# Transposes two tiles behind and loads one step ahead, in three stages of an adaLN block with local attention and a soft mixture

## The reference

```python
h = _layernorm(x) * (1 + ca) + sa
x = x + ga * _L0_attn_ref(h, w_qkv, proj, w_out, b_out)   # window of 7 tokens, ends in out @ w_out + b_out
h = _layernorm(x) * (1 + cb) + sb
x = x + gb * _L0_ffn_ref(h, gamma_x, gamma_slot, slot_embeds, w1, w2)

# _L0_ffn_ref, one batch entry: s = 2048 tokens, d = 1024, e*t = 4096 slots
xn = rms_norm(x, gamma_x)
se = rms_norm(slot_embeds, gamma_slot)
logits = jnp.einsum('bsd,etd->bset', xn, se)
dispatch = jax.nn.softmax(logits, axis=1)                 # over the tokens
slots = jnp.einsum('bsd,bset->betd', xn, dispatch)
processed = jax.nn.gelu(slots @ w1, approximate=False) @ w2
combine = jax.nn.softmax(logits.reshape(b, s, e * t), axis=-1)   # over the slots
out = jnp.einsum('bnd,bsn->bsd', processed.reshape(b, e * t, d), combine)
```

## Time and profile before

| | us |
|---|---|
| two executions | 3873.7 and 4113.04 |
| their median | 3993.37 |
| the profiled execution | 3893.19 |
| span of its slowest core (core 1) | 3891.6 |
| spans of the other cores | 3852.0 to 3878.8 |
| TensorE busy, core 1 | 2578.9 (66%) |
| VectorE, ScalarE busy, core 1 | 966.6 (25%), 626.4 (16%) |

### The profile page before, as it was taken

The page is one execution under the profiler, slowest core; times in us unless marked ns, Lnnn a source line. Parts: engine busy times, 40 slices in busy tenths (PEclk is TensorE's granted clock), DMA queues, the critical chain, the costliest instruction groups (busy, mean ns, idle before and its releaser), DMA issues. The chain is left out here.

```text
span 3891.6 us, 33138 instructions; the slowest of 8 cores (3852.0 to 3891.6 us)
## 1 busy us (share of the span) xinstructions
PE 2578.9 (66%) x11776; PEld 1192.4 (31%) x11776; DVE 966.6 (25%) x1998; ACT 626.4 (16%) x1213; POOL 547.2 (14%) x1021
## 2 busy tenths in 40 slices
PE   5227665656545656665665649888849999667677
PEld 0213222222212222222222213333314444334444
DVE  0543333324652222222222210000041000123232
ACT  0100221211211111111111102222200000122221
POOL 5000000000001111011110115555520000000000
PEclk6558666656767786778777769999969999878788
DMA  9131212002211111111111152222272323132322
GB/s 143 43 68 22 44 38 44 27 33 65 79 54 41 41 41 38 31 41 41 41 39 30 41 99 69 66 65 66 69 141 65 87 65 87 55 119 76 119 76 76
DMA packets 138943, 241.76 MB, mean 62 GB/s; under 512 B 34967, under 2 KB 80279, under 8 KB 137758
## 3 DMA queue, kind: packets, MB, share of 16 engines
q0 software_dynamic: 78864, 138.49, 15.6%
q1 hardware_dynamic: 59918, 101.16, 8.6%
HBM read 201.85 MB, written 83.89 MB: 73 GB/s over the span
## 5 line engine op out<-in xcount | busy, mean ns | idle before, releaser
L1140 PE MATMUL pH<-slots_fm,w_bf 128*128 128x512 bf16 x2048 | 461.0, 385 | 98.2 <-DMA h_sp<-hbuf 54.4
L1227 PE MATMUL pP<-w_bf,hblk 128*128 128x512 bf16 x2048 | 457.7, 385 | 36.8 <-DVE w_bf L1205 20.8
L1054 PE MATMUL pDs<-xn_tm,atm 128*128 128x512 bf16 x1024 | 303.6, 469 | 30.2 <-DVE atm L1045 30.2
L971 PE MATMUL pL<-xn_fm,sefs 128*128 128x512 bf16 x1024 | 289.1, 452 | 50.6 <-DVE sefs L961 50.6
L98 POOL DMA_DIRECT2D h_sp<-hbuf x512 | 272.0, 539 | 287.2 <-ACT hbuf L1151 276.6
L1140 PEld LDWEIGHTS pH<-slots_fm,w_bf 128*128 128x128 bf16 x2048 | 198.1, 99 | 360.8 <-issue 138.7
L1227 PEld LDWEIGHTS pP<-w_bf,hblk 128*128 128x128 bf16 x2048 | 199.3, 98 | 296.3 <-issue 62.0
L98 POOL DMA_DIRECT2D L_sp<-lch x256 | 136.3, 541 | 947.2 <-ACT lch L1005 912.2
L996 ACT ACTIVATE ach<-pL,colC,rscale_all 128x512 bf16<-128x512 f32 x128 | 97.8, 773 | 901.4 <-DVE colC L985 901.4
L1362 PE MATMUL pO<-proc_sm,w_smb 128*128 128x512 bf16 x1024 | 225.4, 381 | 0.9 <-DVE w_smb L1347 0.9
L1036 PE MATMUL pAt<-ident_bf_s,ach 128*128 128x128 bf16 x512 | 52.1, 263 | 239.9 <-DVE atm L1045 239.9
(11 more groups left out here) (184 smaller groups left out, 2484.5 us busy)
## 6 DMA issues: line engine op xcount, KB each, us to landing
L_sp<-lch POOLq DMA_DIRECT2D x256, 128.0 KB, 3.0
h_sp<-hbuf POOLq DMA_DIRECT2D x512, 64.0 KB, 1.8
lblk<-L_sp SPq DMA_DIRECT2D x8, 4096.0 KB, 16.6
se_st<-slot_embeds POOLq DMA_DIRECT2D x32, 512.0 KB, 3.5
wsl<-wmod POOLq DMA_DIRECT2D x96, 128.0 KB, 8.0
xst<-x SPq DMA_DIRECT2D x16, 512.0 KB, 3.2
xrs<-x SPq DMA_DIRECT2D x16, 512.0 KB, 3.8
x_sp<-x2b POOLq DMA_DIRECT2D x16, 512.0 KB, 4.6
```

Source lines behind the costliest of these rows:

```text
L971: e.matmul(pL[nb][:, 0:512], se_fs[buf][:, j * 128:(j + 1) * 128], xn_fm[:, j * N + nb * 512:j * N + (nb + 1) * 512], start=(j == 0), stop ...
L1054: e.matmul(pDs[half][:, 0:512], a_tm[buf][:, nt * 128:(nt + 1) * 128], xn_tm[:, nt * D + half * 512:nt * D + half * 512 + 512], start=(nt ...
L1140: e.matmul(pH[pbase + q][:, 0:512], w1_bf[:, j * HID + hc * 128:j * HID + (hc + 1) * 128], slots_fm[:, j * S + hf * 2048 + q * 512: j * S ...
L1227: e.matmul(pP[2 * (st % 2) + half][:, 0:512], h_blk[blk % 2][:, hc * HBW + st * 128: hc * HBW + (st + 1) * 128], w2_bf[:, hc * D + half * ...
```

## The change

In p1 `emit_xnT` runs two tiles behind the matmuls: tile i emits the transposes of i - 2, and the last two follow behind the loop. Before the matmuls of tile i TensorE now waits for the add of tile i - 2, which read the same PSUM banks; the wait for the transposes of i - 1 had held that before. In p2 the load of slot_embeds is taken out into `p2_se_load`; front(0) issues chunks 0 and 1, and front(sc) chunk sc + 1. In p5 the load of the block of logits is taken out into `lb_load`; an even tile issues block nb + 1 (at the first tile block 0 and block 1). Buffers, tile sizes and arithmetic are as they were.

```diff
--- before.py
+++ after.py
@@ -801,6 +801,8 @@
                         P.wait("sync", "v", x2_mk[i - 2])
                     xrs_mk.append(P.dma("y", x_rs[i % 2][:],
                                         dr["x"][i * 128:(i + 1) * 128, :]))
+                    if i >= 2:
+                        P.wait("tensor", "v", x2_mk[i - 2])
                     for j in range(DJ):
                         P.wait("tensor", "v", fold_mk[j])
                         for half in range(2):
@@ -817,8 +819,8 @@
                             ones_bf[0:1, 0:128],
                             gab_bf[0:1, half * 512:(half + 1) * 512],
                             start=False, stop=True), "t")
-                    if i >= 1:
-                        emit_xnT(i - 1)
+                    if i >= 2:
+                        emit_xnT(i - 2)
                     P.wait("vector", "t", wmk)
                     P.waitm("vector", xrs_mk[i])
                     if i >= 2:
@@ -880,6 +882,7 @@
                         ALU.mult, ALU.mult), "v")
                     m_xn_l.append(m_xn)
 
+                emit_xnT(NT - 2)
                 emit_xnT(NT - 1)
                 m_rsq = P.run("scalar", lambda e: e.activation(
                     rscale_all[:], ssq_se[:], AF.Sqrt), "s")
@@ -937,13 +940,22 @@
             lsp_l = [None] * SC
             rdcol = [None] * SC
 
+            se_mk = [None] * (SC + 1)
+
+            def p2_se_load(sc):
+                if sc >= SC:
+                    return
+                if sc >= 2:
+                    P.wait("gpsimd", "t", sev_m[sc - 2])
+                se_mk[sc] = P.dma("g", se_tm[sc % 2][:],
+                                  dr["slot_embeds"][sc * 128:(sc + 1) * 128, :])
+
             def p2_front(sc):
                 buf = sc % 2
-                if sc >= 2:
-                    P.wait("gpsimd", "t", sev_m[sc - 2])
-                mse = P.dma("g", se_tm[buf][:],
-                            dr["slot_embeds"][sc * 128:(sc + 1) * 128, :])
-                P.waitm("tensor", mse)
+                if sc == 0:
+                    p2_se_load(0)
+                p2_se_load(sc + 1)
+                P.waitm("tensor", se_mk[sc])
                 if sc >= 1:
                     P.wait("tensor", "v", sfold_m[sc - 1])
                 if sc >= 2:
@@ -1274,12 +1286,17 @@
             def p5_lstage(nt):
                 nb, ti = nt // 2, nt % 2
                 p = 4 * (nt % 2)
+                def lb_load(nbx):
+                    if nbx >= NBL or lb_mk[nbx] is not None:
+                        return
+                    if nbx >= 2:
+                        P.wait("sync", "t", ltile_done[(nbx - 2) * 2 + 1])
+                    lb_mk[nbx] = P.dma("y", l_blk[nbx % 2][:].rearrange(
+                        "p (c w) -> p c w", w=NBW),
+                        dr["L_sp"][nbx].rearrange("(c p) w -> p c w", p=128))
                 if ti == 0:
-                    if nb >= 2:
-                        P.wait("sync", "t", ltile_done[(nb - 2) * 2 + 1])
-                    lb_mk[nb] = P.dma("y", l_blk[nb % 2][:].rearrange(
-                        "p (c w) -> p c w", w=NBW),
-                        dr["L_sp"][nb].rearrange("(c p) w -> p c w", p=128))
+                    lb_load(nb)
+                    lb_load(nb + 1)
                 if nt >= 2:
                     P.wait("sync", "v", oev_tile[nt - 2])
                 x2r_mk[nt] = P.dma("y", x2_rs[nt % 2][:],
```

## The result

The changed kernel took a median of 3756.51 us (11 executions, lowest 3752.14); the kernel before, run beside it, 4021.14 (10 executions, lowest 3873.70). The ratio to before is 0.9673, with a 95% interval of 0.9625 to 0.9721: 3.3% faster. Some executions of either kernel have a die that runs at a lower clock and take longer; the ratios leave them out (here they compare seven executions, mean 3758.0, with only two of the kernel before, mean 3885.0), the medians do not. The profiled execution took 3753.25 us, against 3893.19 before.

What follows compares the result with a forecast made beforehand. The prediction took late issue of p5's logits loads, behind stores in SP's queue, as the bound; 95 us (p5), 19 (p1) and 12 (p2) off 3893.19 gave 3767 us, range 3730 to 3880.

Steps and rivals of the forecast that it cites:

- The bound and its cause: p5: every second tile waits for its logits load, issued too late behind a store in SP's in-order queue, not bandwidth.
- The combine stage, 95 us: p5: issuing the logits load a block earlier removes idle time and slow transposes, 95 us, bounds 87 to 102.
- 86.7 us of idle time: p5: TensorE's idle time in 7 waits for the logits load after the first, all expected to go.
- 8.6 us of slower transposes: p5: pT transposes behind a wait take 5.92 us, without one 4.69; 1.2 us saved seven times.
- What is late next: p5: after the change loads have over 30 us of slack, x2rs some 20 us at the start.
- The output projection, 19 us: p1: VectorE's waits for the xn transposes go, 15 x 1.2 + 1.1 = 19 us, bounds 0 and 20.2.
- The slot stage, 12 us: p2: only the second slot_embeds load's wait goes, ScalarE's logit copies being late next; 12 us, bounds 0 and 19.5.
- The sum: Whole kernel: 95 + 19 + 12 = 126 us saved, 3893.19 - 126 = 3767 us; forecast chance 0.70.
- 1 (pair of loads): p5: the first two logits loads share the DMA engines evenly, first block 16 us later; 3783 us, chance 0.09.
- 2 (work slowed by transfers): p5: loads slow the transposes, matmuls and copies beside them, taking back 38 us; 3805 us, chance 0.09.
- 3 (the waits stay): p5: loads are issued earlier but the waits stay, only 31 us won; 3862 us, chance 0.04.
- 4 and 5 (less clock when the gaps close): p5: pO at half clock in 4 of 16 tiles, 3822 us, chance 0.05; in all 16, 3988 us, 0.03.

Runs made afterwards that it cites:

- p5_gpsimd: Kernel before, p5 block load at its old place in the program but issued by GpSimd; p5 443.7 to 446.2 us, six executions 3789.65 to 4081.22 us.
- one_block: Changed kernel, p5 block load one block ahead of its old place instead of two, first two loads not issued together; p5 440.8 to 445.5 us.
- twice: Changed kernel, each 4 MB block of logits in p5 loaded twice into the same buffer; median of 4 is 3783.2 us.
- better_p5: Changed kernel, p5's pW transposes put into the last quarter of the previous tile's pO matmuls, w_smb in two buffers; profiled 3663.26 us.
- better_p2: Changed kernel, p2's ach transposes of chunk sc - 1 moved into the pL matmuls of chunk sc; ratio to before 0.8598, median 3410.73 us.
- better_both: Changed kernel with both the moved ach transposes in p2 and the moved pW transposes in p5; ratio to before 0.8372, median 3340.48 us.

## Why the prediction was right, and where it was wrong

**The bound and its cause.** Right, and shown: the load was issued too late (p5_gpsimd, one_block), bandwidth had room for twice the bytes (twice).

**The combine stage, 95 us.** 92.1 on core 1, for which the sum was made; on the others 79 to 88, as their waits were shorter (78.3 us on core 2). The first of its two terms, 86.7 us of idle time, came whole. The second, 8.6 us of slower transposes, did not: TensorE's busy time for pT on core 1 fell by 1.5 us alone. Before and after (us, PE busy, PEclk, DMA share, GB/s):

```profile
3353.00:3891.00 538.00, 89.91 (x512) 0.80 0.29 94
```

```profile
3300.00:3748.00 448.00, 88.44 (x512) 0.86 0.35 113
```

Another 1.9 us came from the transposes into pW (49.02 to 47.12 us), the remaining 2 from small pieces elsewhere, so that 92 lies near 95 is in part luck. The prediction compared one pT behind a wait (5.92) with one without (4.69) and took the difference for the price of the wait. But with the waits gone every second pT is still 5.7 to 5.8 us long, at a granted clock of 0.60, and blocks did not all come to 25 us. What keeps them slow are the gaps at pW: better_p5 took these away, and every pT after the first two was 3.66 us. Why it is every second one is not shown, as the same gaps lie ahead of both.

**What is late next.** Right: slack everywhere, x2rs among it.

**The output projection, 19 us.** 21.6 to 22.0. The term of 1.2 us for each of 15 tiles was too small: a tile went from 12.73 to 11.4, so 1.4. The copies now begin while the end of xn_tm is still running (963.86, when xn_tm goes to 963.94), which the row of idle time, 1.27, did not hold.

**The slot stage, 12 us.** 10 to 13 where no slow stretch lies; the release by ScalarE came as worked out (matmuls behind lch, 9.65 us).

**The sum.** 126 us expected; 0.0327 of 3885 is 127. That the two agree to 1 us is luck: between the profiled executions the spans of cores 2 to 7 fell by 112 to 126 us, and the slowest span by 140, of which 13 are the slow stretch of core 1.

**Where it was wrong.** Within the sum it is the 8.6 us for slower transposes, of which 1.5 came. The step that failed for the time is the one from the sum to the time, "3893.19 - 126 = 3767 us", with its remark that the median of 3993.4 is the mean of just two. The saving was worked out on one execution and the time given from it, while the median of before, 3993.4, stood 2.6% above it. Measured on more executions the median of before is 4021.14 and the change is worth 0.9673 of what it is applied to: on 4021 that is 3890 us, beyond the top of the range, 3880; and a time of 3767 beside 4021 reads as 6.3% when the mechanism is worth 3.3%. The changed kernel's own median, 3756.5, lies by the 3767. The executions of before, 3873.7 to 4126.3, spread by twice the gain, so a time in us depends more on which of them are drawn than on the change. The range should have been worked out as a ratio, 0.963 to 0.978 by the bounds of the terms (142 and 87 us of 3893), and only then turned into us for each reading of the median. The range did name its weak point: it says that an execution like the one of 4113.0 would lie outside. Four of the ten lie above 4060.

**The rivals.** 1 (pair of loads): out by the landing times, and by one_block. 2 (work slowed by transfers): out by twice. 3 (the waits stay): out, one of eight is left. 4 and 5 (less clock when the gaps close): the opposite happened in p5, 0.80 to 0.86, and 0.95 over the stage in better_p5. The pO steps shown are 13.83 us, with eight cores at work. The limiter of 13/16 (0.81) that the Trainium skill has (TensorE: Matmul & The Clock Gate, Seeing it yourself) would have made them 17.0 us, as an estimate; for p5 the trace disagrees. But the prediction was wrong to leave it at that: the granted clock of 0.81 was in its own trace, in the slow stretch of cores 0 and 1 in p2, and cost them 13 us. The skill has it take the whole die and last as long as the load does. Here it took cores 0 and 1 for some 150 us, while the other six did the same work at 1.00, and in twice all eight for as long.

## What to carry to other kernels

An in-order DMA queue makes a prefetch as late as the store in front of it: look at the queue's own timeline for what stands ahead of a load, and move the load (or give it another queue) before thinking of bandwidth. One step of lead that covers the landing time is enough. And where short gaps hold TensorE's clock down, closing them pays more than the gaps: in better_p5 4 us of gap a block gave 6.5. Last, compare stage by stage and core by core, with the granted clock beside it, before a difference is put down to a change: one stretch at 0.81 weighs as much as the whole part in p2.

## What had not been expected of the hardware

- A stretch of some 150 us in which two cores, or all eight, run matmuls slower (pL step 10.71 us for 8.6, pDs step 10.6 for 9.5), since the granted clock rises to 0.81 in place of 1.00 (0.67 for 0.80 over the window). It costs 13 us here, as much as a whole part of the change, and better_p2 and better_both have it on four and six cores, up to three times on one. What sets it off was not found.
- A 4 MB load issued by GpSimd lands as fast as one issued by SP: a median of 16.8 us in p5_gpsimd, 17.3 in the changed kernel and 16.4 in the one before.
